# Two accumulating transfers in the denominators of a fused four-layer kernel's first attention

## The reference

```python
cp = leaky_relu(einsum('btd,cd->btc', xn, Wc) + bc)
q, k = cp[..., :128], cp[..., 128:256]      # 16 heads of 8
v = cp[..., 256:]                            # 16 heads of 64
scores = einsum('bqhd,bkhd->bhqk', q, k) / sqrt(8)
attn = softmax(scores, axis=-1)
out = einsum('bhqk,bkhd->bqhd', attn, v).reshape(B, T, 1024)
s = leaky_relu(einsum('btv,dv->btd', out, Wo) + bo)
```

## Time and profile before

| | |
|---|---|
| Median of 3 runs | 1073.42 us (1072.49 to 1074.42) |
| Span of the profiled execution, first to last instruction | 1003.7 us |
| The profiled execution's own time | not given beside its page |
| Mean granted TensorE clock | 0.979 |
| First attention, steps | from about 163 to 610 us of the span |

### The profile page before, as it was taken

The page is one execution under the profiler, slowest core; times in us unless marked ns, Lnnn a source line. Parts: engine busy times, 40 slices in busy tenths (PEclk is TensorE's granted clock), DMA queues, the critical chain, the costliest instruction groups (busy, mean ns, idle before and its releaser), DMA issues. The chain is left out here.

```text
span 1003.7 us, 20954 instructions
## 1 busy us (share of the span) xinstructions
PE 920.3 (92%) x7704; PEld 489.4 (49%) x7713; DVE 764.0 (76%) x1332; ACT 538.3 (54%) x901; POOL 597.9 (60%) x533
## 2 busy tenths in 40 slices
PE   5799997999999999999989997899889787799997
PEld 3346563233333333333323233798788444488794
DVE  6978888888888889887888825883689998873514
ACT  1255345666766666666756775443266243274463
POOL 3660425788778777887777893123735886652333
PEclk9999998999999999999999999799999997999999
DMA  9372525111111101111101123567651200243462
GB/s 319 137 225 88 153 64 156 41 51 46 26 52 28 58 24 49 34 55 56 35 26 44 40 67 116 161 193 241 225 156 35 89 22 22 79 142 101 143 196 79
DMA packets 92308, 97.17 MB, mean 97 GB/s; under 512 B 23184, under 2 KB 68624, under 8 KB 91952
## 3 DMA queue, kind: packets, MB, share of 16 engines
q1 hardware_dynamic: 87088, 85.34, 27.8%
q0 software_dynamic: 5120, 10.50, 3.6%
HBM read 70.57 MB, written 24.77 MB: 95 GB/s over the span
## 5 line engine op out<-in xcount | busy, mean ns | idle before, releaser
L255 PE MATMUL ps<-ar 64*64 64x512 bf16 (+5 forms) x5312 | 538.6, 448 | 17.7 <-ACT ar L301 4.3
L255 PEld LDWEIGHTS ps<-ar 64*64 64x64 bf16 (+2 forms) x5312 | 268.5, 137 | 273.4 <-ACT ar L301 92.0
L277 DVE TENSOR_REDUCE small<-ps 128x2 f32<-128x1024 f32 (+2 forms) x276 | 307.2, 1140 | 52.0 <-PE ps L255 50.6
L301 ACT ACTIVATE ar<-ps 128x1024 f32<-128x1024 f32 (+1 forms) x304 | 285.4, 941 | 113.1 <-PE ps L255 106.5
L264 POOL TENSOR_TENSOR psum_sb<-psum_sb,ar 128x1024 f32<-128x1024 f32 x91 | 214.8, 2360 | 57.3 <-DVE on_sb L264 47.1
L264 POOL TENSOR_TENSOR ar<-ar 128x512 f32<-128x512 f32 (+1 forms) x80 | 79.2, 995 | 52.1 <-DVE ar L277 30.0
L323 POOL DMA_INDIRECT gT<-ysort,rt x48 | 46.9, 977 | 98.7 <-issue 97.7
L264 DVE TENSOR_TENSOR ar<-ps,ar 128x256 f32<-128x256 f32 (+4 forms) x56 | 56.2, 1011 | 47.9 <-PE ps L255 43.4
L264 POOL TENSOR_TENSOR psum_sb<-ar 128x1024 f32<-128x1024 f32 x32 | 75.9, 2372 | 16.8 <-ACT ar L301 15.6
L298 ACT COPY ar<-ps 128x256 f32<-128x256 f32 (+1 forms) x84 | 31.8, 386 | 80.8 <-PE ps L255 50.2
L255 PE MATMUL ps<-wA,xnT 128*128 128x512 f32 (+3 forms) x192 | 62.0, 447 | 5.3 <-DVE ar L264 2.7
(11 more groups left out here) (156 smaller groups left out, 1066.0 us busy)
## 6 DMA issues: line engine op xcount, KB each, us to landing
ar<-in_L_up SPq DMA_DIRECT2D x48, 384.0 KB, 4.1
ar<-in_L_b SPq DMA_DIRECT2D x32, 322.0 KB, 3.4
rec_sb<-lscr SPq DMA_DIRECT2D x64, 128.0 KB
scr<-ar SPq DMA_DIRECT2D x48, 128.0 KB, 2.1
ar<-xsort SPq DMA_DIRECT2D x40, 128.0 KB
ysort<-ar SPq DMA_DIRECT2D x40, 128.0 KB, 3.3
ar<-scr SPq DMA_DIRECT2D x32, 112.0 KB
xsort<-xs SPq DMA_DIRECT2D x12, 256.0 KB, 6.2
```

The source lines that it names most:

```text
L255: return self.e.matmul(o, l, r, start=start, stop=stop) if self.e else Nothing()
L277: return self.e.tensor_reduce(o, a, AX.X, op, negate=True) if negate else self.e.tensor_reduce(o, a, AX.X, op)
L301: return self.e.activation(o, a, fn, **kw) if self.e else Nothing()
```

## The change

The change makes these edits:

- Tiles 5 and 6 of a unit are no longer sources of PE's sums. POOL issues two transfers, `dma_add`, that add the tile's slot of `Ps` to `psum_sb` (128 x 1024 fp32, 512 KB each). Tile 5's is issued at POOL's step 7 of the unit, once tile 5 and POOL's (or DVE's) last addition are there. Tile 6's is issued at step 1 of the next unit, behind that unit's first addition, once tile 5's has landed.
- PE's sums have two sources, tile 7 and `psum_sb`, and wait for tile 6's landing. They move from `k = 1` to `k = SUMS = 5`, and with them ACT's copy to `lrow`, SP's transfers (`k = 5` and `k = 10`), DVE's reciprocal (`k = 9`), its multiply (`k = 15`) and the projection (`k = 21`). `osb`'s copy and addition stay at `k = 1`.
- `Ps` has a seventh slot, `ps2_sb`. An exp that overwrites tile 5 or 6 waits for that tile's landing, one that overwrites tile 7 for the sums.
- POOL's additions no longer wait for `scaled`. DVE adds tile 4 of units 27 and later one step earlier.
- The numbers of `SIDE_B` from step 118 on are five higher (at the end fewer, up to 256).

The diff, cut to its core:

```diff
+SUMS = 5
-NP = 6
+NP = 7
...
 SIDE_B = {
-        "30 end0.1 35 end0.0 58 ln.1.1 60 ln.1.0 96 end0.0 138 end0.0 140 ln.1.0 end0.0 142 end0.1 149 ln.1.0 156 "
+        "30 end0.1 35 end0.0 58 ln.1.1 60 ln.1.0 96 end0.0 143 end0.0 145 ln.1.0 end0.0 147 end0.1 154 ln.1.0 161 "
...
+    def dma_add(self, o, i):
+        return self.e.dma_start(o, i, accum_op=ALU.add) if self.e else Nothing()
...
+    Ps = [area(POFF + 1024 * i, 1024) for i in range(NP - 1)] + [ps2_sb[:, :]]
...
     def proj_step(u):
-        return 17 if u % 16 < 14 else 12
+        return 16 + SUMS if u % 16 < 14 else 11 + SUMS
...
-            if k == 1:
+            if k == SUMS:
                 b = island(u) + 1
                 pe.wait_ge(*at("exp", 8 * u + 7))
-                pe.wait_ge(*(at("sums", u, 4) if u < BY_DVE else at("sums_dve", u)))
-                for n, src in enumerate((Ps[:, (8 * u + 5) % NP, :],
-                                         psum_sb[:, 1024 * (u % 2):1024 * (u % 2) + 1024],
-                                         Ps[:, (8 * u + 6) % NP, :], Ps[:, (8 * u + 7) % NP, :])):
+                pe.wait_ge(*at(f"added{u % 2}_in", u, 6))
+                for n, src in enumerate((Ps[(8 * u + 7) % NP], psum_sb[:, 1024 * (u % 2):1024 * (u % 2) + 1024])):
                     for a in range(2):
...
-            if k == 5:
+            if k == SUMS + 4:
                 dve.wait_ge(*at("lcol_in", u))
...
-            if k == 10:
+            if k == SUMS + 10:
                 dve.wait_ge(*at(f"recip_in{m}", u))
...
                     act.wait_ge(*at("pvd", i - NP))
                     k, u = (i - NP) % 8, (i - NP) // 8
-                    act.wait_ge(*(at("sum", u) if k > 4 else at("sums_dve", u) if k == 4 and u >= BY_DVE else
-                                  at("sums", u, max(k, 1))))
+                    act.wait_ge(*(at("sum", u) if k > 6 else at(f"added{u % 2}_in", u, k) if k > 4 else
+                                  at("sums_dve", u) if k == 4 and u >= BY_DVE else at("sums", u, max(k, 1))))
...
+        def add_in(u, k):
+
+            name = f"added{u % 2}_in"
+            pool.wait_ge(*at("exp", 8 * u + k))
+            if k == 5:
+                pool.wait_ge(*(at("sums", u, 4) if u < BY_DVE else at("sums_dve", u)))
+            else:
+                pool.wait_ge(*at(name, u, k - 1))
+            pool.dma_add(psum_sb[:, 1024 * (u % 2):1024 * (u % 2) + 1024], Ps[(8 * u + k) % NP]).then_inc(
+                *landed((name, u, k)))
...
+                if k == 7:
+                    add_in(u, 5)
                 if k == 1:
                     pool.wait_ge(*at("exp", i))
...
-                    if u >= BY_DVE:
-                        pool.wait_ge(*at("scaled", u - 2))
...
-                    if k == 2 and 2 <= u < BY_DVE:
-                        pool.wait_ge(*at("scaled", u - 2))
...
+                if k == 1 and u:
+                    add_in(u - 1, 6)
...
+            add_in(31, 6)
```

More of the change, by code:

```diff
@@ L509, in _program @@
     POFF = KOFF + 3 * 1024
-    assert POFF + NP * 1024 <= AR
+    assert POFF + (NP - 1) * 1024 <= AR
     V0 = area(0, 16384)
@@ L789, in pv @@
                                 V0[r, 1024 * tile + 64 * h:1024 * tile + 64 * h + 64],
-                                Ps[r, i % NP, 512 * a:512 * a + 512], start=kt == 0, stop=kt == 7)
+                                Ps[i % NP][r, 512 * a:512 * a + 512], start=kt == 0, stop=kt == 7)
                 if kt == 7:
@@ L799, in unit_tail @@
             g, hf, pr, c0 = unit(u)
[L800 removed]
+            if k == SUMS:
                 b = island(u) + 1
                 pe.wait_ge(*at("exp", 8 * u + 7))
[L803 to L806 removed]
+                pe.wait_ge(*at(f"added{u % 2}_in", u, 6))
+                for n, src in enumerate((Ps[(8 * u + 7) % NP], psum_sb[:, 1024 * (u % 2):1024 * (u % 2) + 1024])):
                     for a in range(2):
[L808 to L810 removed]
+                        r = 64 * n + 32 * a
+                        ins = pe.mm(ps[r:r + 32, b, :], onesf[:, 0:32], src[:, 512 * a:512 * a + 512])
                 ins.then_inc(*filled(b, ("sum", u)))
@@ L813, in unit_tail @@
                 pi = 2 * (g % 4) + pr
-                b = island(u + 2) if proj_step(u) == 17 else take(ring[0])
+                b = island(u + 2) if proj_step(u) == 16 + SUMS else take(ring[0])
                 pe.wait_ge(*vacant(b))
@@ L859, in attention @@
             pv(255)
-            for x in range(256, 260):
+            for x in range(256, 262):
                 tails(x)
         def tail0():
-            for lo, hi in ((260, 262), (262, 263), (263, 264), (264, 268), (268, 270), (270, 271), (271, 272)):
+            for lo, hi in ((262, 266), (266, 267), (267, 268), (268, 272), (272, 274), (274, 275), (275, 276)):
                 for x in range(lo, hi):
@@ L1305, in attention @@
                     max_pair(*p)
-                if i % 8 == 7 and i // 8 >= BY_DVE:
+                if i % 8 == 6 and i // 8 >= BY_DVE:
                     u = i // 8
@@ L1310, in attention @@
                     dve.wait_ge(*at("sums", u, 3))
-                    dve.tt(a_, a_, Ps[:, (8 * u + 4) % NP, :], ALU.add).then_inc(*up(("sums_dve", u)))
+                    dve.tt(a_, a_, Ps[(8 * u + 4) % NP], ALU.add).then_inc(*up(("sums_dve", u)))
                 tails(i)
@@ L1878, in attention @@
                     k, u = (i - NP) % 8, (i - NP) // 8
-                    act.wait_ge(*(at("sum", u) if k > 4 else at("sums_dve", u) if k == 4 and u >= BY_DVE else
-                                  at("sums", u, max(k, 1))))
-                act.af(Ps[:, i % NP, :], ps[:, b0:b0 + 2, :].rearrange("p a t -> p (a t)"), ACT.Exp,
+                    act.wait_ge(*(at("sum", u) if k > 6 else at(f"added{u % 2}_in", u, k) if k > 4 else
+                                  at("sums_dve", u) if k == 4 and u >= BY_DVE else at("sums", u, max(k, 1))))
+                act.af(Ps[i % NP], ps[:, b0:b0 + 2, :].rearrange("p a t -> p (a t)"), ACT.Exp,
                        scale=SCALE).then_inc(*emptied(("st", i), ("exp", i)))
@@ L2111, in attention @@
                         pool.wait_ge(*at("sum", u - 2))
-                    if u >= BY_DVE:
-                        pool.wait_ge(*at("scaled", u - 2))
-                    pool.tt(a_, Ps[:, (i - 1) % NP, :], Ps[:, i % NP, :], ALU.add).then_inc(*up(("sums", u, 1)))
+                    pool.tt(a_, Ps[(i - 1) % NP], Ps[i % NP], ALU.add).then_inc(*up(("sums", u, 1)))
                 elif 2 <= k <= (4 if u < BY_DVE else 3):
-                    if k == 2 and 2 <= u < BY_DVE:
-                        pool.wait_ge(*at("scaled", u - 2))
                     pool.wait_ge(*at("exp", i))
                     pool.wait_ge(*at("sums", u, k - 1))
-                    pool.tt(a_, a_, Ps[:, i % NP, :], ALU.add).then_inc(*up(("sums", u, k)))
+                    pool.tt(a_, a_, Ps[i % NP], ALU.add).then_inc(*up(("sums", u, k)))
+                if k == 1 and u:
+                    add_in(u - 1, 6)
                 if rows_of(i, 1):
@@ L2418, in attention @@
                 yield
-            for x in range(256, 260):
+            for x in range(256, 262):
                 tails(x)
         def tail0():
-            for lo, hi in ((260, 262), (262, 263), (263, 264), (264, 268), (268, 270), (270, 271), (271, 272)):
+            for lo, hi in ((262, 266), (266, 267), (267, 268), (268, 272), (272, 274), (274, 275), (275, 276)):
                 for x in range(lo, hi):
                     tails(x)
-                if hi == 272:
+                if hi == 276:
                     sp.wait_ge(*at("acc", 31))
```

3 lines of the change are left out of this document (1 added, 2 removed), and 48 rows, old and new, of the table SIDE_B.

## The result

The changed kernel takes **1161.43 us** (median of 4 runs, 1160.72 to 1167.37) against 1073.92 (1072.49 to 1075.01): a ratio of 1.0813, 95% interval 1.0769 to 1.0857. It is 87.5 us slower. The prediction said 1101, with 1058 to 1150 as its range: the sign was right, the size was not.

What follows compares the result with a forecast made beforehand. PE was taken to bound the attention. Window terms +5.1, +1.3, +5.5, +0.8, +8.1 and +7 at the end made +28 us on the span of 1003.7, added to the median 1073.4 for 1101; range 1058 to 1150.

Steps and rivals of the forecast that it cites:

- PE's saving, 0.87 us a unit: PE's sums in the first attention: two of four rounds go, 0.87 us a unit, 28 us over 32 units.
- The moved tails, 0.5 us a unit: Projection and sums move from step 1 to 5; DVE falls behind and PE stalls about 0.5 us a unit.
- Landing, L = 5.0: Time from issue to landing of each 512 KB adding transfer, taken as 5.0 us, between 4.2 and 6.0.
- The transfer may take 4.5: Tile 6's transfer before PE's sums: up to 4.5 us is covered, every microsecond beyond is PE's in each unit.
- POOL, +3.2 us a unit: POOL: two more issues, 2.5 us a unit, plus 0.7 us of tile 5's landing left open.
- The windows: Five stretches of the first attention, of 6, 10, 4, 6 and 5 units, each given its own added time.
- L = 6.0: Same sum with a 6.0 us landing, POOL +4.2 and PE +1.13 us a unit: +61, 1134 us.
- PE's rule: Second and fourth windows: PE-bound units cost -0.37 + 0.5 = +0.13 us each, with a 5.0 us landing.
- End of the attention, +7: Last unit: two landings one behind the other, 10 us less 0.9 of sums; 7 of 9 us reach the end.
- The lost `scaled` waits: POOL no longer waits for DVE's multiply; if they conflict, PE's stall is 1.0 us a unit, but possibly small.
- The signs: Expected evidence: PE's DMA wait 0.5 to 1 us, landing near 5, second-window units 13.2 to 14, POOL over 95%.
- Rival 2: Addition costs the transfer twice or more, landing 6.0 us or above, PE waits 1.5 us every unit: 1134; chance 0.30.

Runs made afterwards that it cites:

- none1: Kernel before, with tiles 5 and 6 left out of PE's sums and nothing moved: 1059.31 us, ratio 0.9849.
- none5: Changed kernel without both accumulating transfers and the waits for them, moved steps kept: 1109.16 us, ratio 1.0292.
- Copy: Changed kernel with plain 512 KB copies in place of the accumulating transfers: 1119.16 us, ratio 1.044.
- before again: Kernel before, unchanged, profiled a second time: 1078.6 us in one run, span 1076.8.
- after_proj17: Changed kernel, transfers kept, with the projection back in front of product 17: 1161.39 us, ratio 1.0849.
- small: Changed kernel with adding transfers of 16 of the 1024 columns (8 KB): 1115.14 us, ratio 1.0419.

## Why the prediction was right or wrong

- **PE's saving, 0.87 us a unit: right.** none1 shows 0.86 in a light unit and 22.7 us over the attention; at the end of the program 16 us are left of it (ratio 0.9849).
- **The moved tails, 0.5 us a unit: this step failed.** I costed DVE's late searches and took the block's place in step 1 to be free. Without any transfer my terms give 32 x -0.37 = -12 us; none5 measured +31. That is 43 of the 59.5 us by which the forecast of +28 was short of +87.5. Measured: none5 to none1 is 35.0 us in the attention, over 1 us a unit, and 48 us in all. The mechanism, for about half of it, was another: the projection and the sums were the cover under which the product banks are emptied. The rows showed it: in the earlier trace rows DVE's `osb` addition starts at 317.08, beside the projection that starts at 316.35 in the earlier trace rows. I had noted that DVE's work lies beside that block, and did not ask which of it PE would wait for once the block is gone. What I did cost, late searches, is small: PE waits 6.3 us for them in none5 and 2.8 in none1.
- **Landing, L = 5.0: mis-sized.** The rest of my +28 was for the transfers, 40 us, and they measured 56 (0.052). Where the next user waited for it, the landing took 4.9 to 7.1 us for tile 5 (median 5.7, 18 cases) and 4.7 to 7.3 for tile 6 (median 5.3, 22 cases). My estimate with each byte read twice was 6.0. Copy against the change shows that it is the addition: 512 KB plain take 87 us of the 16 engines, adding 184, and cost 40 us more of the kernel's time. By the Trainium skill's rule (Collectives: The Full Stack, "The bandwidth ceiling: the fold count and why AG ≠ RS ≠ AR") a reducing transfer reads two sources and is about half as fast. The 2.1 agrees with it in size; the runs do not show what a packet does inside. I took 5.0 as lying between two bounds, though a read of the sum is needed for every addition.
- **"The transfer may take 4.5": about right, but not a free allowance.** The chain through exp 13 is 6.6 + 2.3 us without the landing, in the unit read above. With none1's unit of 12.6 that leaves 3.7 us for it, with none5's 13.85 it leaves 4.9.
- **POOL, +3.2 us a unit: over-priced, and not the bound I named.** An issue is 0.88 us, not 1.25, and POOL's busy time rose by 50.3 us over the five windows (397.4 against 347.1), 1.6 a unit. It is not over 95% busy in the third and fifth windows, but 81 and 71%. What POOL does cost is order: it stands still until tile 5 has landed (25.7 us in 18 units), and carries that wait and its gathers into the chain.
- **The windows.** Forecast with L = 5.0: +5.1, +1.3, +5.5, +0.8, +8.1. Measured from sum to sum: +11.7, +18.7, +13.9, +12.6, +15.3; between the exps of the same steps, which is the fair count: +13.7, +13.9, +15.9, +14.1, +16.7. My own sum with L = 6.0 had 11.1, 11.3, 9.5, 6.8, 13.1: nearer, and below by 22 us in all. The largest misses are the second and the fourth window, where I let PE's rule decide and the tails' price was missing. (My second window has a slip, 103.3 + 32 is 135.3 and not 135.6; it changes nothing.)
- **End of the attention, +7: right in kind, and in size partly by luck.** Between the starts of DVE's last addition and of the sums there were 1.3 us and are now 14.9 (717.38 to 732.26), two landings behind each other, as I wrote, but of 5.5 and 7.3 us where I had 5.0 each. From the last exp to the last sums it is 10.5 us against 3.7, +6.8:

```profile
717.38 1.23 DVE L265 TENSOR_TENSOR psum_sb<-psum_sb,ar 128x1024 f32<-128x1024 f32 x1 [3.09 <-POOL psum_sb L265]
```

```profile
732.26 1.07 PE L256 MATMUL ps<-ar,onesf 128*32 128x512 f32 x2 [6.93 <-DMA psum_sb<-ar]
```

- **The start: nothing missing.** The first sum comes 10.3 us later because four more steps stand before it; the exps of the first steps are at most 1.4 us later than before again.
- **The clock: left out.** With as many matmuls, PE is busy 416.1 us from first to last sum with the change (granted clock 0.96) and 402.8 in none5 (0.99). I had the clock at 1.00 and costed none of it. How much of these 13 us is on the path was not separated.
- **The lost `scaled` waits: nothing to be seen**, neither in the multiply's median (682 ns) nor in DVE's busy time. SP's queue and the seventh slot, costed at nothing, were not tested alone.
- **The signs.** PE's wait for the DMA came, 45.1 us in 22 units, 2 us each where I had 0.5 to 1 in most. The landing was near 5 us at best. Units of the second window took 14.2 to 19.4 us, not 13.2 to 14. POOL over 95% did not come.

As a whole, by ratios: saving -0.015, moved tails +0.044, two plain transfers +0.015, the additions in them +0.037, together +0.081. These shares hold in this order of steps only; after_proj17 shows that the projection's part of the tails (19 us) is worth nothing once the transfers are there. Moving the sums back with the transfers in place was not tried. Rival 2 had the right mechanism for one half of it, and its 1134 lacked the other half. Not settled is what within the plain transfers costs the 16 us: small pays as much, so it isn't bytes, and which of issues, landings in a row and slots it is stays open.

## What to carry to other kernels

Before moving a block off a step, ask what is emptied or finished beneath it: work on the busy engine that "costs" 2.9 us may be the cover for a hand-over of banks that costs 1.2 us when bare. Look for closed chains (slot free, exp, addition, transfer, slot free) and take the longest of them with the engine's own work, not their sum; where a chain through a transfer is the longest, it costs the whole landing in each turn, and relieving the engine beside it gave nothing here. An idle wait that no data asks for may be what keeps two engines off each other: it is tested by removing it alone.

## What the runs showed of the hardware

- An accumulating transfer of 512 KB within SBUF took 4.7 to 7.3 us from issue to its first user, where that waited for it, with an issue of 0.88 us on POOL; a plain one took an issue of 0.55 us, and PE waited for it 14.6 us in the whole attention against 45.1. Its packets took 2.1 times the plain ones' time on the 16 DMA engines (184 and 87 us for 64 transfers).
- A multiply of DVE with two inputs in SBUF took 2812 ns in the median where nothing kept it off POOL's additions and 681 ns where a wait did; an addition of 128x1024 took 3.07 us beside one of POOL's against 1.22.
- Two profiled executions of one kernel differed by 73 us in span (1003.7 and 1076.8), nearly all of it outside the stage studied, with longer waits marked "issue" and "remote". One profile's span may not be the runs'.
- The granted clock in the five stages of the attention was 1.00, 1.00, 1.00, 0.98 and 1.00 before again, and 0.96, 0.99, 0.95, 0.95 and 0.91 with the change, where PE stood idle more.
